# Placing row 0's projection tiles between the normalisations of the four rows

## The chip, the cores and the metric

The kernel runs on one core of a Trainium2 chip. The metric is the device time of one execution in microseconds (us). The engines are called by their names in the profile: PE (TensorE), PEld (its weight loads), DVE (VectorE), ACT (ScalarE), POOL (GpSimd) and SP (SyncE, which issues most DMAs).

## What is computed

Four rows of 512 tokens with 256 channels go through one block: a layer norm with modulation, a Mamba-2 layer, then a second modulated layer norm and a mixture of eight experts. Only the start of the Mamba layer is touched. Cut to that:

```python
mod = (silu(c) @ wmod).reshape(4, 6, 1, -1)
h = layernorm(x) * (1 + ca) + sa                 # ca, sa: two of the six parts of mod
xBCzA = einsum('bld,ed->ble', h, in_proj_w)       # 2112 columns
xBC, z, A_log = xBCzA[..., :1536], xBCzA[..., 1536:2048], xBCzA[..., 2048:]
xBC = silu(depthwise_conv(xBC, taps=4) + bias)    # x, B and C
dt = softplus(A_log)                              # 64 heads, feeds every decay
y_ssm = ssd_chunk_scan(x, -dt, B, C, chunk=128)
out = einsum('bld,ed->ble', (y_ssm + D * x / dt) * silu(z + z_bias), out_proj_w)
x = x + ga * out
# then: layer norm, top 2 of 8 experts, x = x + gb * experts
```

## The kernel before

One list, `program_order()`, holds the steps of the whole program in one order, and each engine walks through this list and issues its own part of every step. The queues of the engines are in order, so where a step stands in the list decides what waits behind it on each engine.

Rows are numbered 0 to 3. A row is four tiles of 128 tokens. The projection of a row gives 16 tiles of 128 columns by 512 tokens: tiles 0 to 3 are x, 4 to 7 and 8 to 11 are B and C (these twelve are convolved), 12 to 15 are z. The program has a start (lines 103 to 108), in which all four rows are normalised, dt and its factors are made for all four rows, and row 0 is projected. Behind it comes a loop over the four rows and their four token tiles, in which the next row is projected in gaps, and then the experts.

The steps of the start that matter here (the numbers of lines are those before the change):

- `("ln1", b)`: DVE normalises row b (line 1290, four instructions) and takes the statistics of row b+1 (lines 1269 and 1272, after waiting for that row's load). PE transposes (line 1617), ACT scales with the modulation and writes hT (line 1082). POOL makes the reciprocal deviations (lines 974 and 975).
- `("mod", 0)` and `("mod", 1)`: the modulation on PE (line 1647), copied by DVE (lines 1332 and 1337). The scaling of hT needs half 0.
- `("proj", 0, m)`: PE multiplies (line 1701, four matmuls in the trace) into one PSUM bank. ACT writes the last convolution tap for a tile m below 12 (line 1141), or the silu of a z tile (line 1146). DVE adds the three older taps with three instructions (line 1313), which read the bank too. ACT's silu of the convolved tile (line 1070) stands behind ACT's part of the next projection tile. DVE takes the older taps of a tile at the next projection step, or behind the step after the projection, whichever comes first.
- `("dt", h)`: PE projects dt for rows 0 and 1 (h = 0) or 2 and 3 (h = 1) with 64-column matmuls (line 1661). It needs hT of these rows.
- `abs`, `exp`, `log`, `factors`, `decays`, `flag`: softplus and the factors made of dt. ACT loads the table of exp (line 1098), and keeps the silus of the convolved tiles back until `flag`. DVE runs lines 1349 to 1353 for each half (`exp`), line 1359 (`log`), lines 1366 and 1369 (`factors`) and line 1374 (`flag`), PE lines 1670 and 1680 to 1690. `flag` makes a register value on which PE waits before it goes on.
- `("rows",)`: PE transposes the gates, ACT copies them (line 1154), and SP sends them through memory and back.
- `("d_dt", 0)`: the reciprocal of dt on DVE (line 1381), then a POOL product (line 982).

The first step of the loop, `tr` (PE line 1627), waits for all twelve silus of row 0.

Which PSUM bank a projection tile of row 0 gets follows from its place in `ROW_0_ORDER` (line 44): banks 0 and 1 in turn for the first places, then banks 0, 1 and 6 in turn (line 215). PE waits at a tile until the tile that had the bank before is read: all three older taps, or the silu of a z tile.

SP issues the loads in the order of lines 808 to 823, behind them a fill of 12 MB with zeros.

Of the kernel before, what the change touches and what calls it, by code (L numbers as in the profile page):

```python
# [26 lines left out]
DI, N_HEAD, HEAD, N_GRP, D_STATE = 512, 64, 8, 8, 64  # L27
# [13 lines left out]
G_BANK = 2  # L41
WARM_UP = 4
WARM_BANK = 7
ROW_0_ORDER = (0, 1, 2, 3, 12, 13, 4, 5, 6, 7, 8, 9, 10, 11, 14, 15)
LEVELS = 8

N_SPARSE = 3
# [48 lines left out]
def program_order():  # L96

    def proj(b, *tiles):
        return [("proj", b, m) for m in tiles]

    z_tiles = range(N_CONV, N_PROJ)

    steps = [("ln1", 0), ("mod", 0), ("ln1", 1), *proj(0, 0), ("ln1", 2), *proj(0, 1), ("ln1", 3),
             ("dt", 0), *proj(0, 2), ("dt", 1), ("abs", 0), ("abs", 1), *proj(0, 3), ("exp", 0), ("exp", 1),
             *proj(0, z_tiles[0]), ("mod", 1), *proj(0, z_tiles[1]), ("log", 0), ("log", 1), *proj(0, 4),
             ("factors", 0), ("factors", 1), *proj(0, 5), ("decays",), ("flag",), *proj(0, 6), *proj(0, 7),
             ("rows",), *proj(0, 8), *proj(0, 9), *proj(0, 10), *proj(0, 11),
             *proj(0, z_tiles[2]), ("d_dt", 0), *proj(0, z_tiles[3])]
    pair_work = pair_steps()
    for slot in range(BATCH):  # L110
# [84 lines left out]
def bank_jobs(step, tail):  # L195
# [15 lines left out]
    if kind == "proj":  # L211
        m = step[2]
        if step[1] == 0:
            n = ROW_0_ORDER.index(m)
            return {step: n % 2 if n < 8 else (0, 1, 6)[n % 3]}
        if step[1] == 1 and m < N_CONV:
            return {step: (0, 1, 7)[m % 3] if m < N_CONV - 1 else 0}
        return {step: m % 2 if m < N_CONV else (m + 1) % 2}
# [41 lines left out]
def adaln_block(nc, x_d, cT_d, wmod_d, win_d, small_d, wo_d, wg1_d, wg2_d,  # L260
                wup_d, bup_d, wdn_d, bdn_d, pairw_d, const_d, route_d, early_d, sel_d, gen_d, out_d, xs_d, ys_d, mod_d):
    STEPS = program_order()
    tail_from = max(n for n, s in enumerate(STEPS) if s[0] in ("out", "norm"))
    bank_of, use_no, used = {}, {}, [0] * 8
# [12 lines left out]
    with ExitStack() as ctx:  # L277
        def sb(name, shape, dt=F32):
            return ctx.enter_context(nc.sbuf_tensor(name, shape, dt))
# [39 lines left out]
        dt = sb("dt", [P, N_TILE, N_HEAD])  # L319
# [6 lines left out]
        flag = sb("flag", [1, 1], I32)  # L326
# [469 lines left out]
        def _(sp):  # L796
# [5 lines left out]
            def load_row(b):  # L802
                sp.dma_start(xin[:, b * TPB:(b + 1) * TPB, :], xr[b]).then_inc(ld_x[b], 16)

            def load_win(name, lo, hi):
                sp.dma_start(win[:, :, lo:hi], win_r[:, :, lo:hi]).then_inc(ld[name], 16)
# [3 lines left out]
            sp.dma_start(cst[:, :], const_d).then_inc(ld["cst"], 16)  # L810
            sp.dma_start(wmod[:, :, 0:2 * DM], wmod_r[:, :, 0:2 * DM]).then_inc(ld["wmod0"], 16)
            sp.dma_start(small[:, :], small_d).then_inc(ld["small"], 16)
            load_row(1)
            load_win("win_x", 0, DI)
            load_row(2)
            load_row(3)
            load_win("win_dt", 4 * DI, N_IN)
            load_win("win_z", 3 * DI, 4 * DI)
            sp.dma_start(early, early_d).then_inc(ld["early"], 16)
            sp.dma_start(sel32, sel_d).then_inc(ld["early"], 16)  # L820
            sp.dma_start(wmod[:, :, 2 * DM:6 * DM], wmod_r[:, :, 2 * DM:6 * DM]).then_inc(ld["wmod1"], 16)
            load_win("win_bc", DI, 3 * DI)
            sp.dma_start(rt[:, :], route_d).then_inc(ld["route"], 16)
            sp.wait_ge(zrow_made, 1)
            n_fill = N_SLOT // P
# [28 lines left out]
            rows = {}  # L854
# [1178 lines left out]
```

## Time and profile before

| | us |
|---|---|
| median of 3 runs | 456.32 |
| lowest, highest | 452.03, 462.3 |
| the profiled execution's own time | 454.92 |
| its span in the profile | 452.7 |

The span is what the hardware profiler shows from the first to the last instruction; 2.22 us of the execution's own time lie around it. A row of a timeline or of the chain begins with its start and its duration in us. In a timeline the brackets hold the idle time of the engine before the row and what ended it.

### The profile page before, as it was taken

What the parts mean: (1) busy time and instruction counts of PE and PEld (TensorE: products, weight loads), DVE (VectorE), ACT (ScalarE), POOL (GpSimd) and SP (SyncE); (2) the same over time, 40 slices, a digit from 0 to 9 for tenths busy, and PEclk for the clock granted to TensorE, in tenths of its full rate; (3) what the DMA queues carried; (4) which work ended last, traced back from release to release, by engine and by line L of the source; (5) the groups of instructions that cost most, each with busy time, mean ns of one, the idle gap of its engine ahead of it and who ended that gap; (6) DMA issues with size and microseconds to landing.
All of it is one profiled execution on the core that took longest, in us unless ns stands there. A gap on an engine that the chain in (4) does not pass through costs nothing.

```text
span 452.7 us, 8779 instructions
## 1 busy us (share of the span) xinstructions
PE 391.1 (86%) x3224; PEld 251.9 (56%) x3224; DVE 289.5 (64%) x624; ACT 166.6 (37%) x291; POOL 138.3 (31%) x170
## 2 busy tenths in 40 slices
PE   7699798888878999798999799776988887988997
PEld 4388342465535556465655465442876776575365
DVE  4733748898894678997658999643643731035566
ACT  1516656542332252342343334022442334354310
POOL 1300200423224243047361208604246100516330
PEclk9859799999988999898999999967998999689999
DMA  8999911200000111002022001106466479997223
GB/s 264 366 385 387 369 66 36 49 13 4 1 2 2 50 25 60 1 2 94 3 72 61 0 3 55 42 2 192 138 196 225 143 236 308 307 301 256 82 70 116
DMA packets 45820, 56.41 MB, mean 125 GB/s; under 512 B 4228, under 2 KB 37676, under 8 KB 45764
## 3 DMA queue, kind: packets, MB, share of 16 engines
q1 hardware_dynamic: 38276, 44.38, 30.0%
q0 software_dynamic: 2304, 6.29, 4.2%
q10 hardware_dynamic: 5184, 4.98, 3.1%
q8 instruction: 36, 0.59, 0.5%
q14 instruction: 20, 0.16, 0.1%
HBM read 32.82 MB, written 22.82 MB: 123 GB/s over the span
## 4 chain that ended last, share of the span: by engine, by line
PE 53%; DVE 27%; issue 7%; DMA 5%; ACT 4%; SPq 2%; POOL 1%; DVEq 0%; ACTq 0%; POOLq 0%
DVE conv L1313 13%; PE ps L1701 13%; PE ps L1757 4%; PE ps L1766 3%; PE ps L1902 3%; PE ps L1920 3%; PE ps L1857 3%; PE ps L1831 3%; PE ps L1780 2%; PE ps L1627 2%; PE ps L1661 2%; DMA hs<-w_pair 2%; PE ps L1818 2%; PE ps L1800 2%; PE ps L1748 2%
## 5 line engine op out<-in xcount | busy, mean ns | idle before, releaser
L1701 PE MATMUL ps<-hT,win 128*128 128x512 f32 x256 | 134.4, 653 | 7.9 <-DVE conv L1313 6.8
L1313 DVE SCALAR_TENSOR_TENSOR conv<-ps,small,conv 128x511 f32<-128x511 f32 x144 | 106.6, 746 | 31.2 <-ACT conv L1141 27.8
L1701 PEld LDWEIGHTS ps<-hT,win 128*128 128x128 f32 x256 | 48.2, 205 | 52.3 <-issue 38.5
L1141 ACT ACTIVATE conv<-ps,small 128x512 f32<-128x512 f32 x48 | 37.2, 775 | 78.1 <-PE ps L1701 78.1
L945 POOL TENSOR_SCALAR rst<-mv 128x1 f32<-128x1 f32 x16 | 3.6, 228 | 133.8 <-DVE mv L1263 133.8
L1070 ACT ACTIVATE conv<-conv 128x512 f32<-128x512 f32 x48 | 29.8, 624 | 29.0 <-DVE conv L1313 29.0
L1056 POOL DMA_INDIRECT conv<-pair_out,ysloti x24 | 24.2, 1008 | 38.9 <-DVE x L1584 25.2
L1857 PE MATMUL ps<-wog,yT 128*128 128x256 f32 x128 | 32.1, 395 | 1.6 <-issue 1.6
L1857 PEld LDWEIGHTS ps<-wog,yT 128*128 128x128 f32 x128 | 24.9, 200 | 11.0 <-issue 8.2
L1627 PE MATMUL ps<-cst,conv 128*128 128x128 f32 x128 | 20.0, 278 | 9.3 <-issue 2.6
L1627 PEld LDWEIGHTS ps<-cst,conv 128*128 128x128 f32 x128 | 14.5, 141 | 21.9 <-issue 14.4
L1037 POOL DMA_INDIRECT pair_rows<-hs,sloti x24 | 24.1, 1006 | 6.9 <-issue 6.9
L1011 POOL TENSOR_TENSOR xv<-xtok,fv 128x512 f32<-128x512 f32 x16 | 17.9, 1116 | 27.2 <-ACT xtok L1197 27.1
L1757 PE MATMUL ps<-conv,hs 128*128 128x128 f32 x152 | 21.7, 290 | 4.9 <-DMA hs<-w_pair 3.9
L1800 PEld LDWEIGHTS ps<-xv,btok 64*64 64x64 f32 x448 | 13.5, 146 | 20.4 <-issue 13.6
L1800 PE MATMUL ps<-xv,btok 64*64 64x64 f32 x448 | 15.7, 237 | 9.4 <-ACT btok L1204 3.4
L1757 PEld LDWEIGHTS ps<-conv,hs 128*128 128x128 f32 x152 | 19.5, 200 | 7.2 <-issue 4.4
L1146 ACT ACTIVATE sz<-ps,small 128x512 f32<-128x512 f32 x16 | 10.9, 684 | 32.9 <-PE ps L1701 20.8
L1766 PE MATMUL ps<-hs,conv 128*128 128x256 f32 x76 | 21.1, 417 | 0.9 <-DVE hT L1570 0.8
L1831 PE MATMUL ps<-xv,gm 64*64 64x64 f32 x512 | 19.2, 227 | 2.2 <-PE ps L1818 0.9
L1831 PEld LDWEIGHTS ps<-xv,gm 64*64 64x64 f32 x512 | 16.9, 140 | 4.5 <-PE ps L1818 4.5
L1171 ACT ACTIVATE conv<-ps,bupt 128x128 f32<-128x128 f32 x38 | 11.9, 364 | 20.3 <-PE ps L1757 20.3
(189 smaller groups left out, 619.0 us busy)
## 6 DMA issues: line engine op xcount, KB each, us to landing
pair_rows<-zrow SPq DMA_DIRECT2D x1, 12288.0 KB, 43.8
hs<-w_pair SPq DMA_DIRECT2D x38, 256.0 KB, 4.1
conv<-pair_rows SPq DMA_DIRECT2D x38, 128.0 KB, 2.6
pair_out<-conv ACTq DMA_DIRECT2D x18, 256.0 KB, 4.6
conv<-x SPq DMA_DIRECT2D x4, 512.0 KB, 7.5
wog<-w_out_T SPq DMA_DIRECT2D x4, 512.0 KB, 3.9
win<-w_in_T SPq DMA_DIRECT2D x2, 512.0 KB, 7.8
hs<-w_mod SPq DMA_DIRECT2D x1, 1024.0 KB, 9.7
```

The costliest lines, as they stand in the source:

```text
L1037: pool.indirect_dma_start(xs_d, bass.IndirectOffsetOnAxis(routed(sloti, b, k, i), 0), hb[b][:, i, :], None, bounds_check=N_SLOT - 1, oob_i ...
L1056: pool.indirect_dma_start(yg[:, n % 4, k, :], None, ys_d[g], bass.IndirectOffsetOnAxis(routed(ysloti, b, k, i), 0), bounds_check=GROUP_TIL ...
L1070: act.activation(dst, dst, ACT.Silu).then_inc(silu_done, 1)
L1141: act.activation(conv[:, b % 2, m, :], bank(step), ACT.Identity, bias=cb[:, m:m + 1], scale=cw[:, m, KSIZE - 1:KSIZE]).then_inc(tap0, 1)
L1313: dve.scalar_tensor_tensor(out=dst, in0=bank(("proj", b, m))[:, 0:SEQ - s], scalar=cw[:, m, KSIZE - 1 - s:KSIZE - s], in1=dst, op0=ALU.mul ...
L1627: ins = pe.transpose(bank(job)[:, tile_cols(j)], conv[:, b % 2, base + j, tile_cols(i)], ident)
L1701: ins = pe.matmul(bank(step), win[:, k, m * P:(m + 1) * P], hT[:, k, b * SEQ:(b + 1) * SEQ], start=(k == 0), stop=(k == KD - 1))
L1757: ins = pe.matmul(bank(step)[:, tile_cols(t % 2)], wt[:, t % W_RING, k * P:(k + 1) * P], hg[:, q % 2, k, tile_cols(t % QUAD)], start=(k == ...
L1766: ins = pe.matmul(bank(step)[:, j * DM:(j + 1) * DM], hq[:, q % 2, tile_cols(t % QUAD)], wt[:, t % W_RING, KD * D_EXP:], start=True, stop= ...
L1800: ins = pe.matmul(ps[64 * par:64 * par + 64, bank_of[job], j * CHUNK:(j + 1) * CHUNK], btok[rows, n % 2, g * 64:(g + 1) * 64], xv[rows, n ...
L1831: last = pe.matmul(ps[rows, bank_of[job], j * CHUNK:(j + 1) * CHUNK], gm[rows, n % 2, par, j * CHUNK:(j + 1) * CHUNK], xv[rows, n % 2, g * ...
L1857: ins = pe.matmul(bank(step)[:, 0:DM], yT[:, n % 2, m, :], wog[:, m, :], start=(m == 0), stop=(m == CT_ - 1))
```

## The change

The start of the step list is written anew. Before, projection tiles 0 and 1 stood between the normalisations, and the other ten convolved tiles behind them. Now tiles 0 to 5 stand between the normalisations, two in each gap, tiles 6, 7 and 8 around the dt steps, and z tiles 12 and 13 go where tiles 9 and 10 stand around. `ROW_0_ORDER` follows, and the first ten places, not eight, now alternate between banks 0 and 1. The load of the x weights goes ahead of row 1's, that of the B and C weights ahead of row 3's, and the z weights behind two small constants.

```diff
-ROW_0_ORDER = (0, 1, 2, 3, 12, 13, 4, 5, 6, 7, 8, 9, 10, 11, 14, 15)
+ROW_0_ORDER = (0, 1, 2, 3, 4, 5, 6, 7, 8, 12, 9, 13, 10, 11, 14, 15)
...
-    steps = [("ln1", 0), ("mod", 0), ("ln1", 1), *proj(0, 0), ("ln1", 2), *proj(0, 1), ("ln1", 3),
-             ("dt", 0), *proj(0, 2), ("dt", 1), ("abs", 0), ("abs", 1), *proj(0, 3), ("exp", 0), ("exp", 1),
-             *proj(0, z_tiles[0]), ("mod", 1), *proj(0, z_tiles[1]), ("log", 0), ("log", 1), *proj(0, 4),
-             ("factors", 0), ("factors", 1), *proj(0, 5), ("decays",), ("flag",), *proj(0, 6), *proj(0, 7),
-             ("rows",), *proj(0, 8), *proj(0, 9), *proj(0, 10), *proj(0, 11),
+    steps = [("ln1", 0), ("mod", 0), *proj(0, 0, 1), ("ln1", 1), *proj(0, 2, 3), ("ln1", 2), *proj(0, 4, 5), ("ln1", 3),
+             *proj(0, 6), ("dt", 0), *proj(0, 7), ("dt", 1), ("abs", 0), ("abs", 1), *proj(0, 8), ("exp", 0), ("exp", 1),
+             *proj(0, z_tiles[0]), ("mod", 1), *proj(0, 9), ("log", 0), ("log", 1), *proj(0, z_tiles[1]),
+             ("factors", 0), ("factors", 1), *proj(0, 10), ("decays",), ("flag",), *proj(0, 11), ("rows",),
              *proj(0, z_tiles[2]), ("d_dt", 0), *proj(0, z_tiles[3])]
...
-            return {step: n % 2 if n < 8 else (0, 1, 6)[n % 3]}
+            return {step: n % 2 if n < 10 else (0, 1, 6)[n % 3]}
...
+            load_win("win_x", 0, DI)
             load_row(1)
-            load_win("win_x", 0, DI)
             load_row(2)
+            load_win("win_bc", DI, 3 * DI)
             load_row(3)
             load_win("win_dt", 4 * DI, N_IN)
-            load_win("win_z", 3 * DI, 4 * DI)
             sp.dma_start(early, early_d).then_inc(ld["early"], 16)
             sp.dma_start(sel32, sel_d).then_inc(ld["early"], 16)
+            load_win("win_z", 3 * DI, 4 * DI)
             sp.dma_start(wmod[:, :, 2 * DM:6 * DM], wmod_r[:, :, 2 * DM:6 * DM]).then_inc(ld["wmod1"], 16)
-            load_win("win_bc", DI, 3 * DI)
```

The line numbers of the changed kernel are lower by one from line 821 on. First DVE, early in the start. Before, row 2's normalisation and row 3's statistics stand ahead of the first older taps, and row 3's normalisation behind one group of them:

```order
L1290 TENSOR_SCALAR xn<-conv,mv1,rst1 128x256 [waits xn_used,var_ready,rstd1_ready] x3
L1290 TENSOR_SCALAR xn<-conv,mv1,rst1 128x256 [waits bank5_full,var_ready,rstd1_ready]
L1269 BN_STATS bns1<-conv 128x6 [waits ld_x3]
L1269 BN_STATS bns1<-conv 128x6 x3
L1272 BN_AGGR mv1<-bns1 128x2 [waits dve_chain] x4
L1313 SCALAR_TENSOR_TENSOR conv<-ps,small,conv 128x511 [waits tap0_written]
L1313 SCALAR_TENSOR_TENSOR conv<-ps,small,conv 128x510 [waits taps_added]
L1313 SCALAR_TENSOR_TENSOR conv<-ps,small,conv 128x509 [waits taps_added]
```

Now the older taps of tile 0 come ahead of row 1's normalisation, and two more groups ahead of row 2's:

```order
L1312 SCALAR_TENSOR_TENSOR conv<-ps,small,conv 128x511 [waits tap0_written]
L1312 SCALAR_TENSOR_TENSOR conv<-ps,small,conv 128x510 [waits taps_added]
L1312 SCALAR_TENSOR_TENSOR conv<-ps,small,conv 128x509 [waits taps_added]
L1289 TENSOR_SCALAR xn<-conv,mv1,rst1 128x256 [waits xn_used,var_ready,rstd1_ready] x3
L1289 TENSOR_SCALAR xn<-conv,mv1,rst1 128x256 [waits bank3_full,var_ready,rstd1_ready]
L1268 BN_STATS bns1<-conv 128x6 [waits ld_x2]
L1268 BN_STATS bns1<-conv 128x6 x3
L1271 BN_AGGR mv1<-bns1 128x2 [waits dve_chain] x4
L1312 SCALAR_TENSOR_TENSOR conv<-ps,small,conv 128x511 [waits tap0_written]
```

Ahead of row 3's normalisation stand five groups of older taps in place of one.

Second, PE around the second part of the modulation (`csil,hs`). Before, the tile behind it is z tile 13, then tile 4, then the first matmul of `factors`:

```order
L1701 MATMUL ps<-hT,win 128x512 [waits hT_ready,ld_win_z,taps_added]
L1701 MATMUL ps<-hT,win 128x512
L1647 MATMUL ps<-csil,hs 128x4 [waits hT_ready,csil_ready,ld_wmod1]
L1647 MATMUL ps<-csil,hs 128x4 x15
L1701 MATMUL ps<-hT,win 128x512 [waits hT_ready,taps_added]
L1701 MATMUL ps<-hT,win 128x512
L1701 MATMUL ps<-hT,win 128x512 [waits hT_ready,ld_win_bc,silu_z_ready]
L1701 MATMUL ps<-hT,win 128x512
L1670 MATMUL ps<-dt,yT 128x512 [waits relu_ready,ld_early,dt_ready]
```

Now tile 9 stands there, behind a wait for z tile 12's silu, then z tile 13, and `factors` waits for the silu of z tile 13:

```order
L1700 MATMUL ps<-hT,win 128x512 [waits hT_ready,ld_win_z,taps_added]
L1700 MATMUL ps<-hT,win 128x512
L1646 MATMUL ps<-csil,hs 128x4 [waits hT_ready,csil_ready,ld_wmod1]
L1646 MATMUL ps<-csil,hs 128x4 x15
L1700 MATMUL ps<-hT,win 128x512 [waits hT_ready,silu_z_ready]
L1700 MATMUL ps<-hT,win 128x512
L1700 MATMUL ps<-hT,win 128x512 [waits hT_ready,relu_ready]
L1700 MATMUL ps<-hT,win 128x512
L1669 MATMUL ps<-dt,yT 128x512 [waits silu_z_ready,ld_early,dt_ready]
```

The wait for the z silu moved ahead of a convolved tile, whose older taps DVE now has to take between the two halves of `log`. There DVE reads:

```order
L1358 TENSOR_TENSOR dt<-conv,ytok 128x512 [waits relu_ready,ln_ready]
L1312 SCALAR_TENSOR_TENSOR conv<-ps,small,conv 128x511 [waits tap0_written]
L1312 SCALAR_TENSOR_TENSOR conv<-ps,small,conv 128x510 [waits taps_added]
L1312 SCALAR_TENSOR_TENSOR conv<-ps,small,conv 128x509 [waits taps_added]
L1358 TENSOR_TENSOR dt<-conv,ytok 128x512 [waits relu_ready,ln_ready]
```

Before, the two instructions that write dt stood next to each other.

## Rows read from the trace of the kernel before

**Rows 1.** Windows over the whole start and the two dt halves, with the columns.
```profile
core 0: us, PE busy (x) PEld busy (x) DVE busy (x) ACT busy (x) POOL busy (x), PEclk, DMA share, GB/s
0.00:82.00 82.00, 68.57 (x235) 39.73 (x235) 47.63 (x108) 40.81 (x63) 8.75 (x25) 0.88 0.78 265
24.00:31.00 7.00, 7.00 (x35) 7.00 (x34) 2.05 (x3) 1.45 (x2) 0.00 (x0) 0.50 1.08 385
34.00:38.00 4.00, 4.00 (x34) 3.76 (x34) 2.25 (x3) 1.82 (x4) 0.00 (x0) 1.00 1.09 388
```
**Rows 2.** The chain that ended last, in order of time, 24 to 53 us.
```profile
24.80 6.72 PE ps L1661 x32
...
34.41 3.52 PE ps L1661 x32
...
41.05 1.28 ACT L1098
...
47.16 5.45 PE ps L1701 x8
```
**Rows 3.** Timeline of DVE, 9 to 38 us.
```profile
9.82 1.41 DVE L1269 BATCH_NORM_STATS2 bns<-conv 128x6 f32<-128x256 f32 x4 [0.31 <-DMA conv<-x]
...
17.43 1.38 DVE L1290 TENSOR_SCALAR xn<-conv,mv,rst 128x256 f32<-128x256 f32 x4 [1.48 <-POOL rst L975]
...
20.04 0.36 DVE L1272 BATCH_NORM_AGGREGATE mv<-bns 128x2 f32<-128x6 f32 x4
...
35.26 2.32 DVE L1313 SCALAR_TENSOR_TENSOR conv<-ps,small,conv 128x511 f32<-128x511 f32 x3 [9.14 <-ACT conv L1141]
```
**Rows 4.** Timeline of DVE, 42 to 82 us.
```profile
43.01 0.43 DVE L1349 TENSOR_SCALAR xtok<-conv 128x512 f32<-128x512 f32 x1 [5.43 <-ACT conv L1098]
...
47.02 0.42 DVE L1349 TENSOR_SCALAR xtok<-conv 128x512 f32<-128x512 f32 x1
...
53.51 0.69 DVE L1366 TENSOR_SCALAR conv<-ps 128x512 f32<-128x512 f32 x1 [3.11 <-PE ps L1670]
...
57.79 0.69 DVE L1369 SCALAR_TENSOR_TENSOR xtok<-ps,conv 128x512 f32<-128x512 f32 x1
...
62.98 0.16 DVE L1374 TENSOR_REDUCE flsum<-ps 128x1 f32<-128x2 f32 x1 [1.02 <-PE ps L1690]
...
70.46 11.21 DVE L1313 SCALAR_TENSOR_TENSOR conv<-ps,small,conv 128x511 f32<-128x511 f32 x15 [1.33 <-ACT conv L1141]
```
**Rows 5.** Timeline of ACT: scaling, evacuations, a z silu, the silus held back.
```profile
12.16 1.45 ACT L1082 ACTIVATE hT<-ps,modT 128x512 f32<-128x512 f32 x2 [6.92 <-DVE modT L1337]
...
17.82 0.78 ACT L1141 ACTIVATE conv<-ps,small 128x512 f32<-128x512 f32 x1 [1.06 <-PE ps L1701]
...
49.42 0.69 ACT L1146 ACTIVATE sz<-ps,small 128x512 f32<-128x512 f32 x1
...
66.00 0.78 ACT L1141 ACTIVATE conv<-ps,small 128x512 f32<-128x512 f32 x1 [2.41 <-PE ps L1701]
...
68.09 1.67 ACT L1070 ACTIVATE conv<-conv 128x512 f32<-128x512 f32 x3
```
**Rows 6.** Timeline of PE: tile 0, decays, the tile behind the flag, the first `tr`.
```profile
15.21 2.56 PE L1701 MATMUL ps<-hT,win 128*128 128x512 f32 x4
...
57.73 1.88 PE L1680 MATMUL ps<-dt,yT 128*128 128x512 f32 x4
...
64.01 3.67 PE L1701 MATMUL ps<-hT,win 128*128 128x512 f32 x8 [1.07 <-DVE flag L1375]
...
82.39 0.66 PE L1627 MATMUL ps<-cst,conv 128*128 128x128 f32 x4 [0.90 <-ACT conv L1070]
```

**Rows 7.** Timeline of ACT and POOL: the gate rows and their fold.
```profile
70.85 0.25 ACT L1154 ACTIVATE scr<-ps 32x128 f32<-32x128 f32 x1
...
88.68 2.36 POOL L1023 TENSOR_TENSOR wog<-wog,gates 128x1024 f32<-128x1024 f32 x1
```
**Rows 8.** DMA issues of the page: KB each, us to landing.
```profile
gates<-mod_rows SPq DMA_DIRECT2D x8, 128.0 KB, 4.2
```

## The prediction

> **What bounds the kernel now.** I read the windows over the start first, then the chain that ended last, then the timelines of DVE, ACT and PE up to the first `tr`. The change touches only the start, so its worth is the shift of the moment at which the loop can begin. That moment is the first transpose of `tr` on PE, at 82.39 us [rows 6], and everything behind it follows in the queues' order. In the first 82 us DVE is busy for 47.6 us and PE for 68.6 us [rows 1]: both have gaps, so what sets the end is the chain. The reader should see three stretches in it. First the loads and normalisations, up to the dt matmuls at 24.80 [rows 2]. Then dt: the first half takes 6.72 us at a granted clock of 0.50, the second 3.52 us at 1.00 [rows 1, 2], and DVE stands idle meanwhile for 9.14 us [rows 3] and then for 5.43 us more [rows 4]. Then a serial chain that hops between ACT, DVE and PE, from the table load at 41.05 [rows 2] to the flag at 62.98 [rows 4], 21.9 us. Behind the flag DVE takes the older taps of six tiles, five of them back to back in 11.21 us [rows 4].
>
> So the idea to judge is this: DVE's twelve groups of older taps, 2.24 us each (11.21 / 5), are the same work in either order. Put early they fill DVE's gaps, and fewer are left behind the flag. But the dt chain then starts later. What counts is whether the later start costs more than the shorter rest gives back.
>
> **The change, part by part.** I walk the new order with the durations of the rows.
>
> *Loads.* DVE starts row 1's statistics when that load lands, at 9.82 [rows 3]. Now 512 KB of weights go ahead of it. At the rate of the loads (385 to 388 GB/s in rows 1, a little less this early, I take 370) that is 0.524 MB / 370 GB/s = 1.4 us, so 11.2. The modulation copies stand behind these statistics on DVE, and ACT's scaling of row 0, which waits for them, began at 12.16 [rows 5], 2.3 us after 9.82. It now begins at 13.5 and ends (1.45 us) at 15.0. Tile 0 before started at 15.21 behind row 1's transposes [rows 6]: the two are equal, so the load order gives nothing early and costs nothing there. The other loads stand in another order with the same bytes; they are hidden by tens of us, since B and C weights are first needed at tile 4, about 30 us in. Bounds of this part: 0 to +1.4.
>
> *Tiles 0 and 1 ahead of row 1.* Tile 0 went from PE 15.21 to its evacuation at 17.82, 2.6 us [rows 5, 6]; from 15.0 that gives 17.6. Evacuation 0.78, older taps 2.32 [rows 3]: DVE is through at 20.7. Only then does it normalise row 1, which it did long before that.
>
> *The normalisations with tiles between.* A normalisation and the next statistics run from 17.43 to 20.04 + 0.36 = 20.40, 3.0 us [rows 3]. DVE now has in a row: row 1 (3.0) to 23.7, taps of tiles 1 and 2 (4.5) to 28.2, row 2 (3.0) to 31.2, taps of 3 and 4 (4.5) to 35.7, row 3 (1.4) to 37.1, taps of 5 to 39.3. PE keeps up at full clock: an evacuation begins 2.0 us after the start of its matmuls (64.01 to 66.00) [rows 5, 6], and each bank is free one group of taps earlier. Row 3's transposes end about 37.6. Tile 6 goes in at 37.6, dt half 0 from 39.3 to 42.9 (3.52), tile 7 (1.8) to 44.6, dt half 1 to 48.1. Tile 8's evacuation is 50.1 to 50.9, a silu (0.6) follows, and the table of exp is loaded at 51.6. Before: 41.05. So the dt chain starts 10.5 us later, with the taps of five more tiles done (0 to 7 in place of 0 to 2), 11.2 us of DVE work. That is an even trade so far. One price in it is worth naming: the DVE gap of 9.14 is gone, yet a gap of 5 us before tile 0's taps takes part of its place, and shorter ones while DVE waits for tiles 7 and for exp.
>
> *The dt chain.* From the table load to DVE's first exp instruction 1.96 us (41.05 to 43.01): 53.5. Exp half 0 with one group of taps runs to the start of half 1 in 4.0 us (43.01 to 47.02): 57.5. The silu of the z tile ended at 49.42 + 0.69 = 50.11 [rows 5], 3.1 us after 47.02: 60.6. Here the new wait bites. Tile 9 may not start on PE before that silu (the second place shown in the order), and behind tile 9 stand z tile 13 and the first matmul of `factors`, behind its older taps the second half of dt. Before, these eight matmuls took 5.45 us from 47.16 [rows 2], as PE had fallen to half clock; I take the same clock now, so tile 9 is evacuated 3.1 us after its start (2.0 at full clock), at 63.8 to 64.6. Its taps end at 66.8, dt half 1 at 67.5. Z tile 13 and its silu end about 67.3, and DVE's `factors` starts about 68.3. Before it started at 53.51 [rows 4], 12.5 us after the table load; now it is 16.7, so the wait costs about 4.2 us. From 53.51 to 57.79 + 0.69 = 58.5 both halves of `factors` took 5.0 us with a group of taps between, which is now behind them; I take 4.1, to 72.4. PE's tile 10 ends at 72.7, decays and flag take 5.25 us (57.73 to 62.98): the flag is at 77.95, 15.0 us later than before.
>
> *The rest.* From the flag to tile 11's evacuation 3.0 us (62.98 to 66.00), 81.0. On ACT the evacuation, a table load and three silus took 3.76 us (66.00 to 68.09 + 1.67 = 69.76) [rows 5], then come the gate rows (0.25) [rows 7], a z tile and the last silu (0.6 each by rows 5, where three silus took 1.67), 1.5 us together: 86.3. DVE's last taps end at 84.1 and hide behind this. So `tr` starts at 86.3, against 82.39: **3.9 us later**. Before, six tiles' taps stood behind the flag; now one, but ACT's backlog of silus stands there in both.
>
> Sum against the profiled execution: 454.92 + 3.9 = 458.8. Its time is 1.4 us under the median of the three runs (456.32), so I give 460.
>
> *The steps moved.* Row 0's gate rows leave ACT at 85.0, not at 71.1 [rows 7]. SP stores them with eight DMAs and fetches them back, 4.2 us for the fetch [rows 8] and, I take, as much for the stores: 93.4. POOL folded them at 88.68, 6.3 us behind `tr`, so would want them at 92.6. The fold comes at most a us late, and POOL has the next tile's scaling queued behind it, which I expect it to reach in time. Cost 0, at worst +1 (if POOL's queue has no slack), or +3.4 if the stores take twice the fetch.
>
> *The clock.* The largest unknown. At half clock a dt half costs 6.72 and not 3.52 us, and a tile's evacuation comes at 3.1 and not 2.0. The trace shows PE busy for 7.00 of 7.00 us at 0.50 in the first dt half [rows 1]: steady work of 64-column matmuls did not bring the clock back, while the 512-column tile behind it did (1.00 in the second dt half). The Trainium skill, "TensorE: Matmul & The Clock Gate", Part 1, says the default is throttled and activity releases it; by that alone dt half 0 would have recovered by itself, and this trace disagrees. By the skill's rule more PE work in the early gaps keeps both dt halves fast; by the row it depends on whether the clock is up when they start. Neither sentence changes the sum, which has both halves at 3.52 because a tile stands right ahead of each. Bounds: 0 for that, +3.2 per half; below, -1.1 if tile 9 runs at full clock.
>
> **The rivals.** *A: slower by over 2%.* The gaps that PE gets between the normalisations (it waits for DVE's taps at tiles 3 and 5 and at the transposes) let the clock fall, and both dt halves run at half clock: 460 + 2 x 3.2 + about 1 for late tiles = 467.5. It decides from the second slow half on. For it speaks that PE went into the first dt half at 0.50 [rows 1], coming from the normalisations; against, that tiles of 512 columns now stand there. *B: faster by over 2%.* The long DVE gap of 9.14 goes and nothing opens: tile 9's wait hides, and the ACT backlog is shorter. Then the start is 9.1 us shorter: 447.2. Against it stands that z tile 12's silu is behind exp and ln of both halves on ACT. *C: nothing measurable.* The wait at tile 9 is covered (-4.2): 456. It would be so if the tiles' DVE work had been late anyway.
>
> **How the numbers follow.** The forecast has 0.52, C 0.26, A 0.14, B 0.08. Two per cent is 9.1 us, about what a measurement of this kernel can tell from no change (its three runs span 10 us): faster is 447.2 or less, slower 465.4 or more. So faster 0.08, same 0.78, slower 0.14. The range goes from 451 (half-way from C to B) to 467 (nearly A).
>
> **What would show it.** Right: the exp table load near 51.6 and the flag near 78; PE idle for some 4 us ahead of tile 9, ended by the z silu; one group of taps between the two dt sums on DVE; the first `tr` at 84 to 88 us, and the loop behind it as long as before. Wrong: dt halves at half clock (A), a `tr` before 80 (B), row 1's statistics starting before 10.5 (the load term), or a difference that arises behind `tr`.

## The result and the profile after

| | before | after |
|---|---|---|
| median of 5 runs | 456.32 us | 460.29 us |
| lowest, highest | 452.03, 462.97 | 459.21, 472.92 |
| first `tr` on PE in the profile | 82.39 | 85.97 |

The ratio after to before is 1.0125, with a 95% interval of 1.0063 to 1.0187. The changed kernel is slower, in these runs by less than 2%. The forecast was 460.0 us and "within 2%". A second set of runs of both kernels gave 1.0186 (1.0073 to 1.0299): slower again, but on which side of 2% it leaves open. Ratios in this text are of the fast runs of each kernel (within 1.5% of its fastest), while medians are of all its runs.

The profiled execution of the changed kernel is its slowest, 472.92 us (the other four: 459.21 to 462.64). Its start is like that of a second profile of the same kernel, and its 10 us too many arise behind it, so I compare the two kernels by the moment of the first `tr`, which repeats well, and not by the spans of single profiles.

The two ratios are 5.7 and 8.4 us of some 454 us, and `tr` moved by 3.6. Their intervals reach down to 2.9 and 3.3 us, so they allow that the shift of `tr` is all there is, but don't prove it. Is there a second difference behind `tr`? DVE's line 1413 writes the first state of each row's scan (it is line 1412 in after). From row 0's to row 1's it is 61.3, 61.1 and 59.9 us in three profiles of before, and 63.5 and 61.4 in two of after. But it is 58.0 and 58.2 us in the experiments e1 and e3 below, which have the steps of after in this stretch. So the new order doesn't make this stretch longer; it scatters.

The windows over the start, with those of [rows 1] and three more:

```profile
core 0: us, PE busy (x) PEld busy (x) DVE busy (x) ACT busy (x) POOL busy (x), PEclk, DMA share, GB/s
0.00:82.00 82.00, 63.30 (x230) 34.99 (x231) 45.27 (x105) 37.55 (x57) 8.48 (x25) 0.90 0.74 254
...
14.00:22.00 8.00, 6.38 (x8) 2.48 (x8) 2.54 (x5) 2.22 (x4) 0.37 (x1) 0.61 1.06 355
22.00:39.00 17.00, 12.52 (x43) 5.71 (x44) 16.68 (x42) 9.70 (x15) 2.52 (x4) 1.00 1.09 386
57.00:61.00 4.00, 0.14 (x1) 0.14 (x1) 3.37 (x8) 2.79 (x4) 0.87 (x2) 0.50 0.42 142
```

From 22 to 39 us the change does what it says: DVE is busy for 16.68 of 17 us. In the same time PE, with tiles between the transposes, keeps a granted clock of 1.00. Before 22 and behind 57 us time is lost. In [rows 1] DVE was busy for 47.63 us of the first 82, now only for 45.27, although it has its taps early.

The timeline of DVE, which answers to [rows 3, 4]; brackets hold the idle time before a row and what ended it:

```profile
11.22 1.41 DVE L1268 BATCH_NORM_STATS2 bns<-conv 128x6 f32<-128x256 f32 x4 [1.67 <-DMA conv<-x]
...
19.39 2.31 DVE L1312 SCALAR_TENSOR_TENSOR conv<-ps,small,conv 128x511 f32<-128x511 f32 x3 [6.22 <-ACT conv L1140]
...
53.71 0.43 DVE L1348 TENSOR_SCALAR xtok<-conv 128x512 f32<-128x512 f32 x1 [5.43 <-ACT conv L1097]
...
65.50 2.32 DVE L1312 SCALAR_TENSOR_TENSOR conv<-ps,small,conv 128x511 f32<-128x511 f32 x3 [4.99 <-ACT conv L1140]
67.73 0.68 DVE L1358 TENSOR_TENSOR dt<-conv,ytok 128x512 f32<-128x512 f32 x1
68.41 0.69 DVE L1365 TENSOR_SCALAR conv<-ps 128x512 f32<-128x512 f32 x1
...
77.89 0.16 DVE L1373 TENSOR_REDUCE flsum<-ps 128x1 f32<-128x2 f32 x1 [1.88 <-PE ps L1689]
...
81.72 2.32 DVE L1312 SCALAR_TENSOR_TENSOR conv<-ps,small,conv 128x511 f32<-128x511 f32 x3 [3.50 <-ACT conv L1140]
```

The gap of 9.14 us in [rows 3] is gone, but 6.22 us stand ahead of tile 0's taps, and 4.99 us between the two halves of `log`, where before nothing stood. Behind the flag one group of taps is left in place of six.

The timeline of PE, which answers to [rows 2, 6]:

```profile
14.79 6.38 PE L1700 MATMUL ps<-hT,win 128*128 128x512 f32 x8 [3.06 <-ACT hT L1081]
...
39.66 3.68 PE L1660 MATMUL ps<-win,hT 128*128 128x64 f32 x32
43.18 1.94 PE L1700 MATMUL ps<-hT,win 128*128 128x512 f32 x4
44.95 3.68 PE L1660 MATMUL ps<-win,hT 128*128 128x64 f32 x32
...
60.87 5.54 PE L1700 MATMUL ps<-hT,win 128*128 128x512 f32 x8 [4.29 <-ACT sz L1145]
67.28 1.10 PE L1669 MATMUL ps<-dt,yT 128*128 128x512 f32 x2 [0.87 <-ACT sz L1145]
...
85.97 0.66 PE L1626 MATMUL ps<-cst,conv 128*128 128x128 f32 x4 [1.55 <-ACT conv L1069]
```

Tile 9 (the row at 60.87) waits for 4.29 us for the silu of z tile 12. This is the new wait. The timeline of ACT shows that silu: it stands behind the work for exp and ln of both halves and a table load of its own, ends at 60.8, and tile 9 starts at 60.87:

```profile
58.83 1.28 ACT L1145 ACT_TABLE_LOAD   x1
60.13 0.69 ACT L1145 ACTIVATE sz<-ps,small 128x512 f32<-128x512 f32 x1
...
64.69 0.78 ACT L1140 ACTIVATE conv<-ps,small 128x512 f32<-128x512 f32 x1 [2.74 <-PE ps L1700]
```

The way to the first `tr` falls into four parts, each the distance between two rows: the start up to the load of exp's table; from there to DVE's first instruction of `factors`; to the flag; and to `tr`. For all runs (the last two columns are the first dt half on PE and the median time, with the number of runs):

| run | to table | to factors | to flag | to `tr` | `tr` at | dt half 0 | time (n) |
|---|---|---|---|---|---|---|---|
| before | 41.05 | 12.46 | 9.47 | 19.41 | 82.39 | 6.93 | 456.32 (5) |
| b_again | 41.35 | 12.89 | 9.47 | 19.42 | 83.13 | 6.68 | 457.27 (3) |
| b_again2 | 40.76 | 12.58 | 9.48 | 19.41 | 82.23 | 6.92 | 451.6 (1) |
| after | 51.76 | 16.65 | 9.48 | 8.08 | 85.97 | 3.68 | 460.29 (5) |
| a_again | 51.77 | 17.29 | 9.47 | 8.08 | 86.61 | 3.68 | 463.17 (3) |
| e1_old_loads | 50.52 | 17.37 | 9.47 | 8.08 | 85.44 | 3.68 | 458.51 (4) |
| e2_new_loads | 38.16 | 12.55 | 9.48 | 19.41 | 79.60 | 3.68 | 452.15 (4) |
| e9_new_loads_again | 37.90 | 12.37 | 9.47 | 19.42 | 79.16 | 3.68 | 457.82 (6) |
| e3_tile9_free_bank | 51.22 | 13.71 | 11.16 | 8.09 | 84.18 | 3.68 | 459.73 (4) |
| e4_tile9_behind_log | 52.12 | 12.20 | 9.48 | 8.08 | 81.88 | 3.68 | 455.71 (4) |
| e7_log_and_old_loads | 50.62 | 12.68 | 9.48 | 8.09 | 80.87 | 3.68 | 459.04 (4) |
| e5_one_tile_earlier | 39.71 | 13.60 | 9.47 | 17.34 | 80.12 | 3.83 | 453.19 (10) |
| e8_one_tile_new_loads | 41.03 | 13.25 | 9.48 | 17.35 | 81.11 | 3.68 | 454.82 (2) |
| e6_two_tiles_earlier | 39.84 | 12.67 | 9.47 | 15.12 | 77.10 | 3.68 | 453.24 (4) |

The kernel before, run beside them, had medians of 460.16 us (7 runs, with e1 to e4), 457.0 (13, with e5 and the two repeats) and 458.78 (11, with e6 to e9). These differ by 3 us for the same kernel, and the stretches of the profiles behind `tr` lie between 365.2 and 384.7 us, with only a loose relation to the start. So for a shift of a few us the table's `tr` is the measure, and a median of four runs is not.

The change in one line of sums: 10.7 later table, 4.2 more to `factors`, nothing to the flag, 11.3 less behind it, +3.6 together.

### The profile page after: what moved, and what is told of

It reads as the page before. It is cut to its first block, busy times and chain, and to the rows that moved or that the text cites. A ratio compares the mean times of both kernels' runs of the same rounds, so it can differ in the third digit from the quotient of the medians.

```text
span 470.7 us, 8779 instructions
## 1 busy us (share of the span) xinstructions
PE 401.3 (85%) x3224; PEld 257.4 (55%) x3224; DVE 288.0 (61%) x624; ACT 167.3 (36%) x291; POOL 138.1 (29%) x170
## 4 chain that ended last, share of the span: by engine, by line
PE 53%; DVE 26%; issue 8%; ACT 5%; DMA 4%; SPq 3%; POOL 1%; DVEq 0%; ACTq 0%; POOLq 0%
PE ps L1700 14%; DVE conv L1312 12%; PE ps L1756 4%; PE ps L1901 3%; PE ps L1765 3%; PE ps L1856 3%; PE ps L1919 3%; PE ps L1830 3%; PE ps L1779 3%; PE ps L1626 3%; DMA conv<-pair_rows 2%; PE ps L1747 2%; PE ps L1817 2%; PE ps L1799 2%; DMA conv<-x 2%
## 5 line engine op out<-in xcount | busy, mean ns | idle before, releaser
L1700 PE MATMUL ps<-hT,win 128*128 128x512 f32 x256 | 137.6, 668 | 14.7 <-DVE conv L1312 6.3
L1856 PE MATMUL ps<-wog,yT 128*128 128x256 f32 x128 | 33.5, 408 | 1.6 <-issue 1.6
L1626 PE MATMUL ps<-cst,conv 128*128 128x128 f32 x128 | 22.2, 301 | 9.4 <-ACT conv L1069 3.0
L1626 PEld LDWEIGHTS ps<-cst,conv 128*128 128x128 f32 x128 | 16.2, 154 | 23.2 <-issue 15.1
L1756 PE MATMUL ps<-conv,hs 128*128 128x128 f32 x152 | 23.2, 304 | 4.2 <-DMA hs<-w_pair 3.1
L1756 PEld LDWEIGHTS ps<-conv,hs 128*128 128x128 f32 x152 | 21.0, 215 | 6.1 <-issue 4.4
L1765 PE MATMUL ps<-hs,conv 128*128 128x256 f32 x76 | 22.5, 437 | 0.9 <-DVE hT L1569 0.8
L1391 DVE TENSOR_TENSOR gm<-ps,cst 128x256 f32<-128x256 f32 x32 | 12.2, 415 | 12.4 <-PE ps L1779 12.4
## 6 DMA issues: line engine op xcount, KB each, us to landing
win<-w_in_T SPq DMA_DIRECT2D x1, 1024.0 KB, 10.5
```

The costliest lines, as they stand in the source:

```text
L1626: ins = pe.transpose(bank(job)[:, tile_cols(j)], conv[:, b % 2, base + j, tile_cols(i)], ident)
L1700: ins = pe.matmul(bank(step), win[:, k, m * P:(m + 1) * P], hT[:, k, b * SEQ:(b + 1) * SEQ], start=(k == 0), stop=(k == KD - 1))
L1756: ins = pe.matmul(bank(step)[:, tile_cols(t % 2)], wt[:, t % W_RING, k * P:(k + 1) * P], hg[:, q % 2, k, tile_cols(t % QUAD)], start=(k == ...
L1765: ins = pe.matmul(bank(step)[:, j * DM:(j + 1) * DM], hq[:, q % 2, tile_cols(t % QUAD)], wt[:, t % W_RING, KD * D_EXP:], start=True, stop= ...
L1856: ins = pe.matmul(bank(step)[:, 0:DM], yT[:, n % 2, m, :], wog[:, m, :], start=(m == 0), stop=(m == CT_ - 1))
```

## The experiments

Two theories stood at the start. One: the wait at tile 9 is what makes the change slower, and the loads do nearly nothing. The other: the loads, which start row 1's statistics 1.4 us later, are the cost, or the wait at tile 9 only takes the place of another one.

**The loads alone, in both kernels.** `e1_old_loads` is the changed kernel with the load order of before, `e2_new_loads` the kernel before with the new one (below, the other loads left out as `...`); `e9_new_loads_again` is e2 once more.

```diff
 load_row(0)
 ...
+load_win("win_x", 0, DI)
 load_row(1)
-load_win("win_x", 0, DI)
 load_row(2)
+load_win("win_bc", DI, 3 * DI)
 load_row(3)
 load_win("win_dt", 4 * DI, N_IN)
-load_win("win_z", 3 * DI, 4 * DI)
 ...
+load_win("win_z", 3 * DI, 4 * DI)
 ...
-load_win("win_bc", DI, 3 * DI)
```

> The new order of steps with the loads in the order of before. My theory: in the new order everything early hangs on row 1's statistics (the modulation copies stand behind them on DVE), so the load of the x weights ahead of row 1 costs 1.4 us there, which the prediction had set against tile 0's old place and called nothing. Row 1's statistics start at 9.8 (11.22 in the changed kernel), the table of exp is loaded near 50.4 (51.76) and the first tr starts near 84.6 (85.97); the time is 1 to 1.5 us below the changed kernel. Rival: the wait moves, the x weights are late for tile 0 and nothing is gained: tr at 86.

> The kernel before with only the new order of loads. My theory: row 1's statistics start at 11.2 and each later normalisation of the old order is 1 to 1.4 us late, so the first tr starts at 83.5 (82.39 before), +1.2 us. Rival: the loads are hidden, tr stays at 82.4 and the time within 0.3 us of before.

Measured: e1 has `tr` at 85.44, between the 84.6 of the theory and the 86 of the rival, and only 0.5 us earlier than after (1.2 earlier than its repeat). The table is loaded 1.24 us earlier, yet then the chain to `factors` takes 17.37 in place of 16.65, since tile 9 and z tile 13 ran at a lower clock (6.26 us against 5.54). The repeat of after has the same (6.17 us, 17.29), so this part scatters with the clock. The load term is +0.5 to +1.2 in the changed kernel, inside its bounds of 0 to +1.4.

e2 was the surprise: the theory had `tr` 1.2 us later. With the new loads in the *old* order of the steps it is 2.8 us earlier (79.60 against 82.39), although row 1's statistics start 1.8 us later, at 11.64. The table shows where: in the first part, above all in the first dt half, 3.68 us and not 6.93. The timeline of PE in e2:

```profile
21.47 1.88 PE L1701 MATMUL ps<-hT,win 128*128 128x512 f32 x4
24.82 1.41 PE L1617 MATMUL ps<-cst,xn 128*128 128x128 f32 x8 [1.47 <-DVE xn L1290]
26.06 3.68 PE L1661 MATMUL ps<-win,hT 128*128 128x64 f32 x32
29.58 1.94 PE L1701 MATMUL ps<-hT,win 128*128 128x512 f32 x4
31.35 3.68 PE L1661 MATMUL ps<-win,hT 128*128 128x64 f32 x32
```

The same rows of before:

```profile
19.14 1.88 PE L1701 MATMUL ps<-hT,win 128*128 128x512 f32 x4
22.98 1.81 PE L1617 MATMUL ps<-cst,xn 128*128 128x128 f32 x8 [1.96 <-DVE xn L1290]
24.59 6.93 PE L1661 MATMUL ps<-win,hT 128*128 128x64 f32 x32
31.31 3.10 PE L1701 MATMUL ps<-hT,win 128*128 128x512 f32 x4
```

and the windows around them in before:

```profile
20.00:23.00 3.00, 1.04 (x4) 0.21 (x2) 2.93 (x10) 1.88 (x4) 1.25 (x2) 1.00 1.05 381
23.00:25.00 2.00, 2.00 (x11) 1.80 (x11) 1.97 (x5) 0.59 (x2) 0.00 (x0) 0.60 1.09 389
25.00:31.00 6.00, 6.00 (x30) 6.00 (x30) 1.08 (x2) 1.13 (x2) 0.00 (x0) 0.50 1.08 384
```

(The chain in [rows 2] has the first half as 6.72 and the second as 3.52, since there a row begins at the end of the one ahead; in a timeline these are 6.93 and 3.68.) The two timelines hold the same instructions in the same order. In both PE stands idle ahead of row 3's transposes, for 1.96 us in before and for 1.47 in e2, at a clock of 1.00. Behind the gap of before the clock falls to 0.50 and stays there for the whole dt half, in e2 it doesn't fall. By these rows the fall costs before 0.4 us at the transposes, 3.25 at the dt half and 1.2 at the tile behind it, 4.8 together. The later statistics take back 1.8, which leaves 3.0 us, near the 2.8 measured.

> The kernel before with only the new order of loads, once more: its first look had both dt halves at 3.68 us and tr at 79.6. My theory: this is not luck, since the kernel before had the slow half in three looks of three; tr within 0.7 us of 79.6 again, and the time 1 to 3 us below the kernel before. Rival: the first dt half is at half clock this time, tr near 84.

The repeat had 79.16 and a dt half 0 of 3.68 again, and none of the three profiles of before has that. This alone would speak for the new loads as the cure. But three more profiles bear on it. e5, e6 and e8, below, differ from before and e2 only behind row 3's transposes: up to there e5 and e6 are the kernel before, and e8 is e2. e8's timeline of PE, with the new loads:

```profile
16.73 2.60 PE L1701 MATMUL ps<-hT,win 128*128 128x512 f32 x4
...
24.49 1.76 PE L1617 MATMUL ps<-cst,xn 128*128 128x128 f32 x8 [1.96 <-DVE xn L1290]
26.05 3.05 PE L1701 MATMUL ps<-hT,win 128*128 128x512 f32 x4
```

Here, with the new loads, the clock falls all the same, and the row at 26.05 is at half clock for the most part. In e6, with the old loads, it doesn't fall. For the eight profiles that share this stretch (a tile takes 1.88 us at full clock and some 3.6 at half):

| profile | loads | tile 0 on PE | gap ahead of row 3's transposes | clock behind it |
|---|---|---|---|---|
| before | old | 2.56 | 1.96 | falls |
| b_again | old | 3.26 | 1.96 | falls |
| b_again2 | old | 2.75 | 1.96 | falls |
| e5 | old | 3.16 | 1.96 | falls |
| e6 | old | 3.62 | 1.19 | stays |
| e2 | new | 3.62 | 1.47 | stays |
| e9 | new | 3.52 | 1.66 | stays |
| e8 | new | 2.60 | 1.96 | falls |

So the clock stays up in two of three profiles with the new loads and in one of five with the old ones. That the loads cure dt half 0 isn't shown. What the fall does go with, in all eight, is tile 0. Where tile 0 ran at half clock to its end or nearly so, PE is late, its gap is shorter, and the clock stays up for dt. Where the clock rose during tile 0, PE waits for the full 1.96 us, and the clock falls. What is shown is the price: `tr` is 2.6 to 4.0 us earlier in the two profiles with the new loads and the clock up than in the three of before. A shorter total time is not shown (457.82 us over six runs of e9, before beside it 458.78).

**The wait at tile 9.** `e3_tile9_free_bank` gives tile 9 bank 0, which tile 8's older taps have left by then, so that it doesn't have to wait for z tile 12's silu. `e4_tile9_behind_log` puts tile 9 behind z tile 13 and `log`, where tile 4 stood before. With this e4 also changes the banks of tiles 9 and 13.

```diff
+            if m == 9:
+                return {step: 0}
```

```diff
-ROW_0_ORDER = (0, 1, 2, 3, 4, 5, 6, 7, 8, 12, 9, 13, 10, 11, 14, 15)
+ROW_0_ORDER = (0, 1, 2, 3, 4, 5, 6, 7, 8, 12, 13, 9, 10, 11, 14, 15)
-  *proj(0, z_tiles[0]), ("mod", 1), *proj(0, 9), ("log", 0), ("log", 1), *proj(0, z_tiles[1]),
+  *proj(0, z_tiles[0]), ("mod", 1), *proj(0, z_tiles[1]), ("log", 0), ("log", 1), *proj(0, 9),
-            return {step: n % 2 if n < 10 else (0, 1, 6)[n % 3]}
+            return {step: n % 2 if n < 12 else (0, 1, 6)[n % 3]}
```

> The changed kernel with tile 9 in bank 0, so that PE no longer waits for z tile 12's silu at it. My theory (the new wait at tile 9 is what costs the 4 us): PE starts tile 9 near 58 and not at 60.87, but ACT evacuates it only behind z tile 12's silu and two small casts, near 62.0 and not 64.69; DVE's taps 2.7 us earlier, factors near 66 (68.41), tr near 83.6, about 2.3 us less than the changed kernel. Rival (the bank wait is covered by ACT's queue and the half clock): tr within 0.5 us of 85.97.

> The changed kernel with z tile 13 ahead of tile 9 and tile 9 behind both halves of log, as tile 4 stood before. My theory: from the table load to factors on DVE it is again 12.5 us and not 16.7, so with the table load at 51.76 factors starts near 64.3 and tr near 82, 4 us below the changed kernel and level with before: time 456. Rival (the loss lies in the early part, DVE's 6.2 us gap ahead of tile 0's taps): the chain keeps its length and tr stays near 86.

In e3 tile 9 starts 3.55 us earlier on PE, and `factors` begins at 64.93 in place of 68.41; 0.5 us of this stood ahead of the table already, as row 1's load landed earlier (10.67 against 11.22). The stretch from the table to `factors` is 2.9 us shorter, 13.71 for 16.65, and still 1.3 us longer than in before. What is left stands on DVE, which has to wait for tile 9's taps between the two halves of `log`, 2.14 us in e3 and 4.99 in after:

```profile
62.10 2.32 DVE L1314 SCALAR_TENSOR_TENSOR conv<-ps,small,conv 128x511 f32<-128x511 f32 x3 [2.14 <-ACT conv L1142]
```

And 1.7 us are lost again between `factors` and the flag, 11.16 us in place of 9.48, where the timeline of PE in e3 shows a tile at half clock:

```profile
57.32 5.08 PE L1702 MATMUL ps<-hT,win 128*128 128x512 f32 x8 [2.28 <-DVE conv L1314]
63.28 1.10 PE L1671 MATMUL ps<-dt,yT 128*128 128x512 f32 x2 [0.87 <-ACT sz L1147]
66.49 1.58 PE L1671 MATMUL ps<-dt,yT 128*128 128x512 f32 x2 [2.12 <-DVE xtok L1370]
67.86 3.14 PE L1702 MATMUL ps<-hT,win 128*128 128x512 f32 x4
```

The row at 67.86 is tile 10, 3.14 us where e4, below, took 1.88. A gap of 2.12 us stands in front of the matmuls ahead of it. `tr` is 1.8 us earlier than in after (the theory had 2.3), 1.3 of it behind the table.

In e4 both the wait for the silu and the taps between the halves of `log` are gone, and the clock stays up: 12.20 us from the table to `factors`, as in before, and `tr` at 81.88, 4.1 us ahead of after. The timeline of PE in e4:

```profile
58.23 5.20 PE L1700 MATMUL ps<-hT,win 128*128 128x512 f32 x8 [2.28 <-DVE conv L1312]
63.26 1.02 PE L1669 MATMUL ps<-dt,yT 128*128 128x512 f32 x2
65.89 1.10 PE L1669 MATMUL ps<-dt,yT 128*128 128x512 f32 x2 [1.61 <-DVE xtok L1368]
66.83 1.88 PE L1700 MATMUL ps<-hT,win 128*128 128x512 f32 x4
```

So the 4.2 us of the change are the place of tile 9, and e3 splits them: 2.9 us go with the wait for the bank alone, and the rest, by DVE's row in e3, with the taps that stand between the halves of `log`. With the silu of z tile 12 where it is (60.13 in after), a step that needs its bank can't come before 60.8, whatever stands there.

**Both repairs together.** `e7_log_and_old_loads` is e4 with the load order of before.

> The changed kernel with tile 9 behind both halves of log and the loads in the order of before: both suspected costs taken away at once. tr was 86.0 and 86.6 in the changed kernel, 85.4 with the old loads alone and 81.9 with tile 9 behind log alone. My theory: the two add, with the loads worth their full 1.4 us now that no z silu stands ahead of factors: table load near 50.5, tr near 80.4. Rival (they overlap as in the kernel with only the old loads, worth 0.5 us): tr near 81.4.

80.87, between the two figures: the old loads give 1.0 us here, 1.5 ahead of the table and 0.5 given back behind it. So the rest of the change, with no wait at tile 9 and the old loads, is 1.5 us ahead of the kernel before, which has the slow dt half in its profile.

**The repeats.** `b_again` and `b_again2` are the kernel before, `a_again` is the changed one.

> The kernel before once more, unchanged. The trace of before has the first dt half at half clock (6.72 us), the kernel with only the loads moved has it at full clock (3.5 us). My theory: which of the two an execution gets hangs on when the clock happens to be down, so another execution of the same kernel may have the first tr either at 82.4 (first dt half at half clock) or 3 us earlier, near 79. Rival: the kernel before always pays the half clock there (tr at 82.4 again), and it is the moved loads that cure it.

> A third look at the same kernel, for the same question: tr near 82.4 or near 79, by the first dt half at 6.7 or 3.5 us.

> The changed kernel once more, unchanged. My theory: its start has a tile of 512 columns ahead of each dt half and does not depend on that luck: both halves at 3.5 us and tr at 86.0 within 0.7 us. Rival: it varies as the kernel before does, tr anywhere from 83 to 90.

`tr` came at 82.39, 83.13 and 82.23 in the three profiles of before, at 85.97 and 86.61 in the two of after. Their distance, 2.8 to 4.4 us, is well above the 0.9 us within a kernel. The repeats fit the rival of the first expectation (before always pays half clock), but the table of eight profiles above shows the same early steps both ways. The first dt half had half clock in all three of before, in neither of after. PE waited at tile 9 for 4.29 and 5.28 us.

**Less of the change.** If the gain is the clock of dt half 0, one tile ahead of it should do, without a table that comes 10 us later. `e5_one_tile_earlier` is the kernel before with each tile from tile 2 on one place earlier: tile 2 goes ahead of dt half 0, tile 3 between the halves. `e6_two_tiles_earlier` has tiles 2 and 3 there. z tiles 12 and 13 stay where they stood. Of the edits only this part of the list is shown. The later tiles move up too, `ROW_0_ORDER` follows, and the banks from the ninth place on are dealt anew (0 and 1 in turn for ten places, then 0, 1, 6).

```diff
 ...
-  *proj(0, 1), ("ln1", 3), ("dt", 0), *proj(0, 2), ("dt", 1),
+  *proj(0, 1), ("ln1", 3), *proj(0, 2), ("dt", 0), *proj(0, 3), ("dt", 1),
 ...
```

and in e6

```diff
 ...
-  *proj(0, 1), ("ln1", 3), ("dt", 0), *proj(0, 2), ("dt", 1),
+  *proj(0, 1), ("ln1", 3), *proj(0, 2, 3), ("dt", 0), *proj(0, 4), ("dt", 1),
 ...
```

> The kernel before with one tile more ahead of the first dt half (tile 2 there, tile 3 between the halves, tile 4 behind them, and so on), loads as before. My theory: the extra tile costs 1.7 us of PE ahead of dt, but its older taps fall into DVE's gap of 9 us, so one group of 2.24 us fewer is left behind the flag; and the 512-column tile brings the clock back for dt half 0 in every execution. Table load near 40.3 to 42, tr near 79.4, 3 us below the profiled kernel before. Rival (DVE's gap is not what binds, dt half 0 stays slow): table load at 43, tr at 82.

> The kernel before with two tiles more ahead of the first dt half (tiles 2 and 3), loads as before. The kernel with one more had its first tr at 80.1, from a table load at 39.7. My theory: the second extra tile costs 1.7 us of PE ahead of dt and takes 2.2 us of DVE work from behind the flag: table load near 41.5, tr near 79.6, within 0.7 us of the kernel with one. Rival (each tile moved ahead pays in full): tr near 78.

The timeline of PE in e5:

```profile
22.96 1.41 PE L1617 MATMUL ps<-cst,xn 128*128 128x128 f32 x8 [1.96 <-DVE xn L1290]
24.20 3.47 PE L1701 MATMUL ps<-hT,win 128*128 128x512 f32 x4
27.46 3.83 PE L1661 MATMUL ps<-win,hT 128*128 128x64 f32 x32
```

and in e6:

```profile
22.74 1.41 PE L1617 MATMUL ps<-cst,xn 128*128 128x128 f32 x8 [1.19 <-DVE xn L1290]
23.98 3.93 PE L1701 MATMUL ps<-hT,win 128*128 128x512 f32 x8
27.75 3.68 PE L1661 MATMUL ps<-win,hT 128*128 128x64 f32 x32
```

In e5 the gap is that of before, 1.96 us, and again the clock falls behind it: tile 2 takes 3.47 us where 1.88 is full clock. But it is the tile that pays 1.6 us now, and the 64-column matmuls behind it run in 3.83. `tr` comes at 80.12, 2.3 us before that of before, and here the total follows: 453.19 us, a ratio of 0.9925 (0.9867 to 0.9984). That is faster than before, by less than 2%.

In e6 `tr` is at 77.10, 5.3 us before that of before and below both figures of the expectation (79.6 and 78). Another group of taps is gone from behind the flag (15.12 against 17.34), as expected. But the second tile costs nothing like 1.7 us ahead of the table (39.84 against 39.71), since the clock did not fall in this profile: eight matmuls took 3.93 us, where e5's four took 3.47. As e6 and e5 have the same steps up to there, this is a draw and not a merit of the second tile. With e5's loss of 1.6 us at its tile, my estimate for e6 is 78.7. There is one profile of each. The total time of e6 is known from four runs only, from 444.59 to 459.64 us, which isn't enough to tell it from before or from e5.

`e8_one_tile_new_loads` is e5 with the new loads. If these only cure dt half 0, they are of no use where a tile cures it already.

> The kernel with one tile more ahead of dt, with the new order of loads. The new loads alone took tr of the kernel before from 82.4 to 79.6, since the first dt half then ran at full clock. My theory: that is all they give; with a 512-column tile ahead of dt the clock is up anyway, and what is left of the new loads is their 1.4 us on row 1: tr near 81.5 against 80.1. Rival (the moved loads help by themselves): tr near 78.

81.11, near the 81.5 of the theory, and 1.0 us later than e5, with a fall of the clock in both. So where the clock did the same in both of a pair, the new loads cost 0.5 to 1.2 us: after against e1, e4 against e7, e8 against e5. Only e2 and e9 gain, and there the clock did not do the same as in before.

## Why the prediction was right

The forecast of the time, 460.0, and of the first `tr`, 86.3, came out at 460.29 and at 85.97 and 86.61. That the time came within 0.3 us is luck, as medians of one kernel differ by 3 us; the parts of the shift are not. Step by step:

| step | predicted | after |
|---|---|---|
| row 1's statistics | 11.2 | 11.22 |
| tile 0 starts on PE | 15.0 | 14.79 |
| tile 0's taps done | 20.7 | 21.7 |
| dt halves | 3.52 each, as the chain counts | 3.68 each in the timeline, which is the same |
| table of exp | 51.6 | 51.76 |
| z silu ends | 60.6 | 60.8 |
| tile 9's evacuation starts | 63.8 | 64.69 |
| `factors` | 68.3 | 68.41 |
| flag | 77.95 | 77.89 |
| `tr` | 86.3 | 85.97 |

- **Both have the same shape.** Five groups of taps moved ahead of the chain (11.3 us less behind the flag; the forecast, 86.3 less 77.95, has 11.1) for a table 10.7 us later (10.5), and 4.2 us more to `factors` (4.2). e4 and e3 show that this last term is tile 9's place: with the tile behind `log` the chain is 12.20 us again and `tr` is 4.1 us earlier, and the wait for the bank alone is 2.9 of it. Rival C, where the wait is covered, falls with it.
- **Rival A** (both dt halves at half clock) didn't come, in none of 11 profiles with another order or other loads. **Rival B** needed the gaps to close. DVE has one of 6.22 us and one of 4.99.
- **The gate rows' way through memory cost nothing.** The timeline of POOL in after has the fold waiting for 1.20 us for the gates, at 92.28 (93.4 forecast), and then idle time of its own, 3.83 us, before the next work:

```profile
92.28 2.36 POOL L1022 TENSOR_TENSOR wog<-wog,gates 128x1024 f32<-128x1024 f32 x1 [1.20 <-DMA gates<-mod_rows]
98.46 1.08 POOL L1010 TENSOR_TENSOR xv<-xtok,fv 128x512 f32<-128x512 f32 x1 [3.83 <-ACT xtok L1196]
```

  With stores of twice the fetch the prediction's own figures put the fold at 97.6, 5.0 us late, where it says +3.4. It didn't come to that.

- **What was less right: tile 0.** I took 2.6 us for it, the figure of before. It ran at half clock (granted 0.61 from 14 to 22 us), and the gap ahead of its taps is 6.22 us, not 5, so these were done 1.0 us late. By the table of exp only 0.2 of it was left, in part since a normalisation with statistics and two groups of taps took 7.3 us on DVE and not the 7.5 of my rounded terms. Tile 9 had the same luck: it was evacuated 0.9 us late, and `factors` came on time because DVE went from dt to `factors` without the 0.8 us that I had left there. The gap ahead of exp stayed at 5.43 us, as in before; I had called it shorter than 5.
- **What the prediction had not seen: in the old order the clock of dt half 0 is a draw.** "0 to +1.4" for the loads holds where the clock does the same (+0.5 to +1.2). But with the new loads in the kernel before and the clock up at dt (e2 and e9) `tr` is 2.6 to 4.0 us earlier, which is outside those bounds, and the prediction took the slow half of its one trace for a fixed term. By the table, against the old order with the new loads and the clock up (e2, e9), the new order of the steps costs 6.4 to 7.5 us and not 3.6. The "even trade" of tiles against the dt chain was even only because before paid half clock there, 4.8 us by the rows above. In the new order dt half 0 was fast in six profiles of six (after, a_again, e1, e3, e4, e7), with either order of loads.
- **The clock.** The prediction had both halves fast "because a tile stands right ahead of each". In all nine profiles with a 512-column tile there, e5 and e8 with a tile partly at half clock among them, dt half 0 took 3.68 to 3.83 us. By the Trainium skill, "TensorE: Matmul & The Clock Gate", Part 1, the default is throttled and activity releases it. The rows of e5 agree: the clock fell as PE began the tile and was full again some 0.3 us into the dt half (3.83 us against 3.68). Those of before don't: there PE was busy with 64-column matmuls for 6.00 of 6.00 us at 0.50, and the two repeats have the same.

Why the clock falls behind the gap of 1.96 us in five profiles and not behind 1.19 to 1.66 us in three, I have not tested by itself; the length of the gap, the moment at which the clock had risen and the place of the gap in time changed together. In a_again and e1 a gap of 1.83 us, ahead of row 1's transposes, had no fall behind it either (transposes in 1.41 us, a tile in 1.88).

## What to carry to other kernels

Work that is moved ahead of a serial chain is worth what it takes from behind the chain, less what it delays in front. One tile moved there made the start 2.3 us shorter, and two 5.3, of which some 1.6 are a luckier clock. The change, with more of them in front, made it 3.6 longer, 4.2 of it the place of tile 9 behind ACT's silu, and without that (e4, e7) it was still no shorter than with one tile. Where a tile may have to wait for a PSUM bank that another engine reads late, look up when that reader runs before you put the tile there. Try each part of a change with several parts alone in the kernel before. And before you call a part that gains there a cure, look at every other profile that shares the steps up to that point: here two of two had the gain, and a third with the same steps up to there (e8) did not.

## What I had not expected of the hardware

- The clock of PE differed between profiles with the same instructions up to that point: 32 matmuls of 64 columns took 6.68 to 6.93 us in three profiles of before and 3.68 in both of e2 and e9. In e6 the clock stayed up where e5 had it fall, and in e8 it fell where e2 had it stay.
- In these three profiles a fully busy PE stayed at a granted 0.50 for the 6 us from 25 to 31 us; the second dt half, behind a tile of 512 columns, ran in 3.68 to 3.93.
- With starts that repeat within 0.9 us, the rest of the same program took 367.1 to 375.4 us in three profiles of before, and 372.6 and 384.7 in two of after. In the longer one of after the granted clock is 0.82 from 270 to 360 us, 0.92 in the other.
